# Sixteen output stores issued by ScalarE instead of SyncE in a four-layer graph network kernel

## The chip, the core and the metric

The kernel runs on one core of a Trainium2 chip. A core has TensorE (PE, matmuls; its weight loads are listed as PEld), VectorE (DVE), ScalarE (ACT), GpSimd (POOL) and SyncE (SP), which here only issues DMAs. Each engine works through its own instructions in the order of the program and waits on semaphores for the others. SP and ACT can both issue DMAs; their issuing sides are listed as SPq and ACTq. The metric is the device time of one execution in microseconds (us).

## What is computed

Sixteen graphs of 512 nodes with 128 features go through four attention layers with one shared adjacency matrix. Each layer's result is added to its input and normalised over the features:

```
x = _layernorm(x + _L0_gnn_ref(x, adj, ...))   # 4-head dot-product attention, masked
x = _layernorm(x + _L1_gnn_ref(x, W, a, adj))  # additive (GAT) attention
x = _layernorm(x + _L2_gnn_ref(x, adj, adj[None], ...))  # 8-head GAT with a prior
x = _layernorm(x + _L3_gnn_ref(x, adj, ...))   # MLP, GAT without mask, MLP, GAT with mask
return x                                        # (16, 512, 128) float32
```

The graphs do not depend on each other. Everything is float32 except the two masks.

## The kernel before

A graph's 512 nodes lie as 128 partitions x 4 blocks (C = 4). A layer is cut into stages, for instance `l0_exp` (one exponential of a 128x512 tile of scores) or `l3_norm` (the last normalisation of a graph, four ACTIVATEs of 128x128 at L811). The order of all stages on each engine is written out in the table ORDER: two characters a step, the stage's letter from STAGES and the graph's number in hexadecimal. So K5 in ACT's list is `l3_norm` of graph 5. Several graphs are under way at once, in different layers; PE's list is the densest. A stage waits for what it reads, and for buffers and PSUM banks that it overwrites.

SP's list has loads of a graph's input (`x_load`, L419, tile x_in), the write of a small row table to DRAM (`l2_rows`, L427), eight loads for each graph that spread one row of it over all partitions (`l2_spread`, L434, tile row, five buffers), which DVE reads in `l2_p` (L1230), and until now one `store` for each graph (L423, 256 KB from tile x4 to the output). The store waits for the semaphore l3_x, which the fourth ACTIVATE of `l3_norm` raises:

```
sp.wait_ge(*sig("l3_x", g, 1))
sp.dma_start(out_v[g.i], g.of(x4)[:, :, :]).then_inc(g.of(stored), 16)
```

Tile x4 has two buffers. ACT's `l3b_v` writes one for graph g once the store of graph g - 2 has landed. The program ends when SP has seen all stores land.

The PE stages named below, with what they wait for: `l0_pv` (L522) needs ACT's `l0_t` (L776); the stages at L572 need ACT's three small exponentials (L801 to L803); the projections at L554 need ACT's copy of the transposed input (L748); L616 needs ACT's copy at L834; the scores at L503 need banks that ACT or DVE has emptied. A stage named "warm" (L701) is two matmuls without use in front of a stage that would otherwise find PE idle.

Of the kernel before, what the change touches and what calls it, by code (L numbers as in the profile page):

```python
# [30 lines left out]


STAGES = {
# [55 lines left out]
        "l4i5l4v2a7D1w2w2E1E1b7x2m4x2x2d6x2d6n4d6e6o4d6o4j5e6e6d6e6y2d6c7d6p4F1e6d6r3e6e6K0e6f6f6d6d6d6d6A2H1"
        "H1I1J1t3A2A2A2B2C2d6u3d6l5r4v3e6l5e6d6e6d6e6e6D2w3e6w3f6e6m5x3x3x3x3n5E2E2o5o5K1e6y3d7r4d7d7p5d7f6e7"  # L90
        "A3e7d7e7d7e7d7e7g6A3e7d7h6A3i6A3e7B3e7C3i6t4d7f7d7f7d7F2d7e7e7e7a8e7j6b8f7u4d7c8d7e7d7H2e7H2e7I2d7J2"
        "r5v4e7l6f7l6D3w4w4x4x4m6x4E3x4E3n6o6g7o6K2d8r5d8y4d8h7e8d8e8i7e8i7d8e8d8e8d8a9F3A4p6d8t5e8j7A4d8d8d8"
        "A4d8A4e8b9e8f8u5e8B4e8C4e8v5e8l7l7H3H3f8I3f8J3c9d8d8d8d8r6e8m7e8e8e8D4w5w5f8x5x5x5x5n7E4E4o7o7y5g8K3"
        "r6h8d9aad9i8d9e9i8F4p7d9A5d9e9j8e9d9e9d9A5e9baA5d9e9t6A5B5C5d9H4d9e9u6H4e9d9e9l8e9l8e9I4cav6J4f9d9f9"
        "r7m8e9D5f9w6w6n8E5E5x6x6o8o8x6d9x6d9d9e9d9e9y6e9e9daF5dadar7dap8f9K4eaeaeaeadafadaabdaeadaeag9H5daA6"
        "H5h9daA6dai9I5daA6i9eaJ5eaeaA6B6C6dar8dabbeadaeafaeadaeaeafaeaeacbj9t7faD6E6E6u7v7dbdbw7l9w7dbgal9x7"
        "dbx7F6x7x7ebebebhaebK5dbm9r8y7dbn9dbiao9ebo9dbebiaebdbebdbfbdbdbA7dbp9A7dbjaA7dbA7dbebt8ebB7ebC7ebfb"
        "fbebebebebfbu8laH6lav8acH6I6J6r9bcmaD7w8gbw8E7naE7hbccoax8x8x8x8iboaibK6y8dcjbdcr9dcpadcececececaddc"
        "dcA8dcF7ecdcA8A8ect9ecA8ecB8C8dcdcdcdcH7u9H7lbbdeclbecI7ecdcecdcJ7v9rafcdcecmbecfcecD8fcw9dcw9E8nbE8"
        "ecx9x9fcobobx9x9K7y9cdgcrahcpbicicaeddA9ddedddjcddedF8ededA9ddA9ddedddddedbeededA9ddtaddedddfdddB9H8"  # L100
        "C9ualcH8lcedvaedI8edfdJ8ddddddrbfdddedmcededD9edwawafdncxaxaocK8ocxaxaE9E9cegdF9yarbpchdididafdeH9de"
        "dedeAaH9eeI9eeJ9eeeeAaAadeAadejddeeetbdeeebfeecffedeBadeCaeedeubrceeldeevbeedeeeldfefeDawbwbEadeEade"
        "mdeexbeexbnddexbdexbeeK9eeoddfoddfdfdfrcdffedfefdfefdfefefeftcefgeefybefdfdfpdhedfdfieFaieAbucdfjeAb"
        "dfvcdfdfAbffAbBbCbHaefefHaefIaefJaleleffffefefefrdefmeDbKaffnewcwcoeoexcxcxcxcEbEbycgfrdhfpeififFbjf"
        "ActdAcHbudHbAclfIblfAcvdJbBcCcremfnfofofDcwdwdEcEcxdxdxdxdFcreydpfKbteHcueAdAdveAdAdBdCdHcIcJcrfDdwe"
        "weEdEdxexexexeyeFdrfKctfAeAeAeAeBeCeHdHdufIdJdvfDewfwfEeEeKdxfxfxfxfFeyfHeAfAfAfAfBfHeCfIeJeDfEfEfKe"
        "FfHfHfIfJfKf",
    "dve":
        "00a0b0b0b0b0c000b020b030b040b050c0001000b060b0a1b0b0c0b0b0b0b0c0b1b1b1b1c1d0e0b1b1b1b1c1f0b1b1g0b1h0"
        "b1i0b1c1b1b1b1c1a2b2j0b2b2b2k0c2d1l0e1b2b2n0b2n0b2n0c2f1n0b2b2b2o0b2g1c2h1i1o0b2b2p0b2q0b2c2j1a3k1l1"  # L110
# [33 lines left out]
        "jfpeqeretdvcwcxcpfqfrfvdwdxdtevewexetfvfwfxf",  # L144
    "sp":
        "a0001000a1300000a2a3f0a4g0g0g0g0g0g0g0g0f1g1a5g1g1g1g1g1g1g1f2a6g2g2g2g2g2g2g2g2f3g3g3a7g3g3g3g3g3g3"
        "f4g4g4l0g4g4g4g4g4g4l1f5g5a8g5g5g5g5g5g5g5a9l2f6g6g6g6g6g6g6g6g6aal3f7g7g7g7g7g7g7g7g7f8g8l4abg8g8g8"
        "g8g8g8g8acl5f9g9g9g9g9g9g9adg9g9l6fagagagagagagagagaael7fbgbgbgbgbgbgbgbgbl8affcgcgcgcgcgcgcgcgcl9fd"
        "gdgdgdgdgdgdgdgdlafegegegegegegegegefflbgfgfgfgfgfgfgfgflcldlelf",
}  # L150
BANK_OF_USE = (
    "01234567012345670157021635635437504632017465312704635120743152047320641752306754172305647301526743021654723106"
# [55 lines left out]
def build_program(nc, x, adj, w, out):  # L208
    use = bank_uses()

    with ExitStack() as ctx:
        def sb(name, shape, dt=F32):
            return ctx.enter_context(nc.sbuf_tensor(name, shape, dt))

        def pair(name, shape, dt=F32, n=2):
            return [sb(f"{name}_{q}", shape, dt) for q in range(n)]
# [79 lines left out]
        x4 = pair("x4", [P, C, D])  # L296
        e4 = sb("e4", [P, C, D])
# [9 lines left out]
        stored = [sem(f"stored{q}") for q in range(2)]  # L307
# [44 lines left out]
        def emptied(stage, g, k=0):  # L352
            return bank_read[use[stage, k, g.i][0]]
# [17 lines left out]
        out_v = out.rearrange("b (p c) d -> b p c d", c=C)  # L371
# [13 lines left out]
        def _(sp):  # L385
# [32 lines left out]
                    sp.wait_ge(*took("l0_y", g, back=2))  # L418
                sp.dma_start(g.of(x_in)[:, :, :], x_v[g.i]).then_inc(g.of(x_loaded), 16)  # L419

            def store(g, k):
                sp.wait_ge(*sig("l3_x", g, 1))
                sp.dma_start(out_v[g.i], g.of(x4)[:, :, :]).then_inc(g.of(stored), 16)  # L423

            def l2_rows(g, k):
                sp.wait_ge(*sig("l2_turned", g, 1))
                sp.dma_start(g.of(line2).rearrange("r (q s) -> q r s", s=BLOCK), turned2[:, :]).then_inc(signal["l2_rows"], 16)  # L427
# [284 lines left out]
        def _(act):  # L712
# [175 lines left out]
            def elu_first(n, e, parts):  # L888

                def f(g, k):  # L890
                    for c in range(parts):
                        act.wait_ge(*took(n + "_o", g, c))
                    act.activation(e[:, :, :], e[:, :, :], ACT.Exp, scale=-1.0).then_inc(signal[n + "_ea"], 1)  # L893
                return f

            def elu_second(n, e):
                def f(g, k):
                    act.wait_ge(*sig(n + "_ea", g, 1))
                    act.activation(e[:, :, :], e[:, :, :], ACT.Exp, bias=neg_one[:, 0:1]).then_inc(signal[n + "_eb"], 1)  # L899
# [23 lines left out]
            def l2_old(g):  # L923
# [509 lines left out]
```

## Time and profile before

| | us |
|---|---|
| three runs, median (lowest to highest) | 1078.31 (1078.24 to 1078.61) |
| the profiled execution, its own time | 1080.22 |
| its span, first to last instruction | 1078.4 |
| PE busy | 1024.1 (95%) |
| PE weight loads busy | 760.1 (70%) |
| DVE busy | 914.3 (85%) |
| ACT busy | 771.2 (72%) |
| POOL busy | 272.7 (25%) |

The profile is of one execution. A busy engine may still be one that waits between pipelined instructions, and idle time of an engine that does not set the pace costs nothing. In a row of the timeline the first number is the start in us from the span's start, the second the time until the row's last instruction ends; "x4" means that four instructions are merged in it, and square brackets give the idle time before it and what ended that.

### The profile page before, as it was taken

The numbers are of one execution on the slowest core, as the hardware profiler recorded it, in microseconds if no ns is written. First come the engines' busy times: TensorE is split into PE (matmuls) and PEld (weight loads), VectorE is DVE, ScalarE is ACT, GpSimd is POOL, SyncE is SP. The second block draws the span as 40 slices with busy tenths as digits, with TensorE's granted clock in tenths as the row PEclk, the third lists the DMA queues.
The fourth block names the chain that finished last, engine by engine and source line by source line (L and its number), as shares of the span: only waits on it lengthen the run. The fifth ranks groups of instructions, "written<-read, shape, count | busy, mean of one in ns | idle before, by whom it ended". The sixth has DMA issues, their size and how long they took to land. (4 is left out here: it accounts for less than half of the span.)

```text
span 1078.4 us, 26660 instructions
## 1 busy us (share of the span) xinstructions
PE 1024.1 (95%) x9189; PEld 760.1 (70%) x9189; DVE 914.3 (85%) x2533; ACT 771.2 (72%) x2029; POOL 272.7 (25%) x606
## 2 busy tenths in 40 slices
PE   7989999999999999999999999999999999899985
PEld 5667767667677777868577776777676777666784
DVE  4656999998999988999899799989899798988543
ACT  3979858775777788768886977868867875544543
POOL 1012414131323224222212332223213232220101
PEclk9999999999999999999999999999999999999998
DMA  4000212202020200202030031112020021020000
GB/s 127 2 11 12 90 29 63 70 21 76 16 78 14 90 11 21 80 22 79 2 100 11 12 90 56 35 33 69 21 80 2 25 67 60 30 72 19 11 11 20
DMA packets 30468, 46.81 MB, mean 43 GB/s; under 512 B 6912, under 2 KB 9216, under 8 KB 30336
## 3 DMA queue, kind: packets, MB, share of 16 engines
q1 hardware_dynamic: 29472, 44.84, 13.4%
q8 instruction: 76, 1.25, 0.5%
q14 instruction: 56, 0.46, 0.1%
q10 hardware_dynamic: 864, 0.26, 0.1%
HBM read 40.64 MB, written 4.46 MB: 42 GB/s over the span
## 5 line engine op out<-in xcount | busy, mean ns | idle before, releaser
L1230 DVE SCALAR_TENSOR_TENSOR P<-row,t2e,mask_t 128x512 f32<-128x512 f32 x512 | 355.9, 755 | 11.2 <-PE bank L608 10.4
L766 ACT ACTIVATE probs<-probs,neg_max 128x512 f32<-128x512 f32 x256 | 186.7, 732 | 35.6 <-DVE neg_max L1046 35.6
L1038 DVE CUSTOM_DVE_ANT_0 probs<-bank,mask_add 128x512 f32<-128x512 f32 x256 | 169.5, 677 | 20.4 <-PE bank L503 19.8
L776 ACT ACTIVATE probs_t<-bank 128x512 f32<-128x512 f32 x256 | 151.0, 610 | 12.7 <-PE bank L511 12.2
L511 PE MATMUL bank<-ident,probs 128*128 128x128 f32 x1024 | 142.7, 277 | 5.1 <-ACT probs L766 3.1
L511 PEld LDWEIGHTS bank<-ident,probs 128*128 128x128 f32 x1024 | 114.0, 141 | 37.5 <-ACT probs L766 19.9
L811 ACT ACTIVATE x<-x,shift_l,rstd_l 128x128 f32<-128x128 f32 x256 | 105.3, 487 | 38.9 <-POOL shift_l L1368 38.9
L608 PE MATMUL bank<-P,GH 128*32 128x512 f32 x1024 | 116.4, 595 | 4.5 <-issue 3.2
L653 PE MATMUL bank<-t,l_P 128*128 128x258 f32 x512 | 119.8, 383 | 1.0 <-DVE l_P L1152 0.9
L1353 POOL TENSOR_TENSOR rstd_l<-mv_l,ln_eps 128x4 f32<-128x4 f32 x64 | 16.1, 252 | 384.0 <-DVE mv_l L1092 383.8
L653 PEld LDWEIGHTS bank<-t,l_P 128*128 128x128 f32 x512 | 93.8, 190 | 16.7 <-issue 2.5
L1386 POOL TENSOR_TENSOR t<-t 128x128 f32<-128x128 f32 x128 | 55.5, 465 | 169.1 <-ACT t L803 169.1
L608 PEld LDWEIGHTS bank<-P,GH 128*32 128x32 f32 x1024 | 31.7, 109 | 67.1 <-issue 64.7
L503 PE MATMUL bank<-head_k,head_q 32*128 32x512 f32 x512 | 72.7, 638 | 1.2 <-ACT probs_t L776 0.8
L1361 POOL TENSOR_TENSOR rstd_l<-rstd_l,neg_half 128x4 f32<-128x4 f32 x64 | 70.5, 1102 | 4.2
L522 PE MATMUL bank<-probs_t,v 128*32 128x128 f32 x2048 | 68.1, 275 | 0.4 <-DVE row_max L1038 0.4
L522 PEld LDWEIGHTS bank<-probs_t,v 128*32 128x32 f32 x2048 | 52.7, 109 | 21.7 <-issue 11.7
L584 PE MATMUL bank<-t,l_P 128*128 128x129 f32 x512 | 62.3, 276 | 0.0
L584 PE MATMUL bank<-t,l3b_P 128*128 128x130 f32 x512 | 61.5, 276 | 0.8 <-DVE l3b_P L1136 0.8
L584 PEld LDWEIGHTS bank<-t,l_P 128*128 128x128 f32 x512 | 59.4, 192 | 4.0 <-DVE l_P L1136 1.9
L584 PEld LDWEIGHTS bank<-t,l3b_P 128*128 128x128 f32 x512 | 59.2, 191 | 2.7 <-DVE l3b_P L1136 1.3
L644 PE MATMUL bank<-w_fc,h_t 128*128 128x258 f32 x256 | 60.2, 383 | 0.9 <-DVE row_max L1038 0.9
(168 smaller groups left out, 1922.5 us busy)
## 6 DMA issues: line engine op xcount, KB each, us to landing
row<-line SPq DMA_DIRECT2D x128, 256.0 KB, 3.7
x_in<-in_x SPq DMA_DIRECT2D x16, 256.0 KB, 2.8
out<-x SPq DMA_DIRECT2D x16, 256.0 KB, 2.0
l_P<-in_adj SPq DMA_DIRECT2D x4, 256.0 KB, 5.2
w_fc<-in_L_gnn_W_fc SPq DMA_DIRECT2D x1, 256.0 KB, 4.2
P<-in_L_gnn_a_fc SPq DMA_DIRECT2D x1, 256.0 KB, 3.5
line<-turned SPq DMA_DIRECT2D x16, 16.0 KB
w_cat<-in_L_gnn_W SPq DMA_DIRECT2D x2, 64.0 KB, 4.1
```

The costliest lines, as they stand in the source:

```text
L503: pe.matmul(ps("l0_s", g, HEADS0 * c + h)[:, :], g.of(head_q)[rows, c * P:(c + 1) * P], g.of(head_k)[rows, :], start=True, stop=True)\
L511: last = pe.transpose(ps[:, j * P:(j + 1) * P], probs[m // HEADS0 % 2][:, m % HEADS0, j * P:(j + 1) * P], ident[:, :])
L522: last = pe.matmul(ps[DH0 * h:DH0 * (h + 1), 0:P], g.of(v0)[:, j, DH0 * h:DH0 * (h + 1)], probs_t[c % 2][:, h, j, :], start=(j == 0), stop ...
L584: last = pe.matmul(ps[:, c * width:(c + 1) * width], gat[n]["P"][:, j, (2 * k + c) * P:(2 * k + c + 1) * P], g.of(t)[:, j, 2:2 + width], s ...
L608: last = pe.matmul(ps[DH0 * h:DH0 * (h + 1), :], g.of(GH)[:, j, (GROUP2 * q + h) * W2:(GROUP2 * q + h) * W2 + DH0], P2[:, h, j, :], start= ...
L653: last = pe.matmul(ps[:, 0:HID + 2], gat["l3"]["P"][:, j, c * P:(c + 1) * P], g.of(t3)[:, j, 2:4 + HID], start=(j == 0), stop=(j == C - 1))
L766: act.activation(e, e, ACT.Exp, bias=neg_max[:, m:m + 1], scale=SCALE0, accum_out=g.of(den0)[:, m:m + 1])\
L776: act.activation(probs_t[c % 2][:, h, :, :].rearrange("p j n -> p (j n)"), ps("l0_t", g, m)[:, :], ACT.Copy)\
L811: last = act.activation(y[:, c, :], y[:, c, :], ACT.Identity, bias=shift[n][:, c:c + 1], scale=rstd[n][:, c:c + 1])
L1038: dve.tensor_tensor_reduce(probs[c % 2][:, h, :], ps("l0_s", g, m)[:, :], mask_add[:, c, :], 1.0, -3.0e38, ALU.add, ALU.max, row_max[:, m: ...
L1230: last = dve.scalar_tensor_tensor(P2[:, h % GROUP2, j, :], row(g, h)[:, :], g.of(t2e)[:, j, h:h + 1], mask_t[:, j, :], ALU.max, ALU.mult)
L1361: pool.tensor_tensor(rstd[n][:, :], rstd[n][:, :], neg_half[:, :], ALU.pow)\
```

## The change

The stage `store` leaves SP's list and comes into ACT's as letter L, for each graph directly behind that graph's K (`l3_norm`). Its wait and its DMA are the same, but ACT now executes them. All other steps of all lists keep their order.

```diff
 STAGES = {
-    "sp": "0:adj_load 1:late_loads 3:out_load a:x_load f:l2_rows g:l2_spread l:store",
+    "sp": "0:adj_load 1:late_loads 3:out_load a:x_load f:l2_rows g:l2_spread",
...
-           "I:l3b_ea J:l3b_eb K:l3_norm",
+           "I:l3b_ea J:l3b_eb K:l3_norm L:store",
...
-            def store(g, k):
-                sp.wait_ge(*sig("l3_x", g, 1))
-                sp.dma_start(out_v[g.i], g.of(x4)[:, :, :]).then_inc(g.of(stored), 16)
...
+            def store(g, k):
+                act.wait_ge(*sig("l3_x", g, 1))
+                act.dma_start(out_v[g.i], g.of(x4)[:, :, :]).then_inc(g.of(stored), 16)
```

SP at the first two stores, graphs 0 and 1, before. The names in brackets are the semaphores that a step waits for; p2_made tells that DVE has used a row buffer:

```order
L427 DMA line_0<-turned 4x32x32 [waits l2_turned]
L434 DMA row<-line_0 128x512 [waits p2_made,l2_rows]
L434 DMA row<-line_0 128x512 [waits p2_made]
L423 DMA out<-x_0 128x512 [waits l3_x]
L434 DMA row<-line_0 128x512 [waits p2_made] x6
L423 DMA out<-x_1 128x512 [waits l3_x]
L427 DMA line_1<-turned 4x32x32 [waits l2_turned]
```

And now:

```order
L423 DMA line_0<-turned 4x32x32 [waits l2_turned]
L430 DMA row<-line_0 128x512 [waits p2_made,l2_rows]
L430 DMA row<-line_0 128x512 [waits p2_made] x7
L423 DMA line_1<-turned 4x32x32 [waits l2_turned]
L430 DMA row<-line_1 128x512 [waits p2_made,l2_rows]
```

Both waits for l3_x are gone from between the row loads (the function's removal also moves the line numbers by four).

ACT around `l3_norm` of graph 5 (near 603 us in the trace), before:

```order
L811 ACTIVATE x_1<-x_1,shift_l,rstd_l 128x128 [waits l3_shift]
L811 ACTIVATE x_1<-x_1,shift_l,rstd_l 128x128 x3
L766 ACTIVATE probs,den_1<-probs,neg_max 128x512 [waits neg_max0]
L811 ACTIVATE x_1<-x_1,shift_l,rstd_l 128x128 [waits l1_shift]
L811 ACTIVATE x_1<-x_1,shift_l,rstd_l 128x128 x3
L834 ACTIVATE o_raw<-bank 128x512 [waits bank_written0]
```

And now:

```order
L807 ACTIVATE x_1<-x_1,shift_l,rstd_l 128x128 [waits l3_shift]
L807 ACTIVATE x_1<-x_1,shift_l,rstd_l 128x128 x3
L900 DMA out<-x_1 128x512 [waits l3_x]
L762 ACTIVATE probs,den_1<-probs,neg_max 128x512 [waits neg_max0]
L807 ACTIVATE x_1<-x_1,shift_l,rstd_l 128x128 [waits l1_shift]
L807 ACTIVATE x_1<-x_1,shift_l,rstd_l 128x128 x3
```

One DMA stands between the normalisation and the exponential that followed it at once, and it waits for the normalisation in front of it.

ACT at `l3_norm` of graph 14 (near 1057 us), before:

```order
L790 ACTIVATE t_0<-bank 128x2x130 [waits bank_written2,bank_written1]
L811 ACTIVATE x_0<-x_0,shift_l,rstd_l 128x128 [waits l3_shift]
L811 ACTIVATE x_0<-x_0,shift_l,rstd_l 128x128 x3
L801 ACTIVATE l3b_R<-l3b_ss 128x4 [waits bank_read4,l3b_dd]
L802 ACTIVATE l3b_b<-l3b_dd 128x4
```

And now:

```order
L786 ACTIVATE t_0<-bank 128x2x130 [waits bank_written2,bank_written1]
L807 ACTIVATE x_0<-x_0,shift_l,rstd_l 128x128 [waits l3_shift]
L807 ACTIVATE x_0<-x_0,shift_l,rstd_l 128x128 x3
L900 DMA out<-x_0 128x512 [waits l3_x]
L797 ACTIVATE l3b_R<-l3b_ss 128x4 [waits bank_read4,l3b_dd]
L798 ACTIVATE l3b_b<-l3b_dd 128x4
```

Here graph 14's store has come in front of the three small exponentials of graph 15, the last graph.

## Rows read from the trace of the kernel before

**Rows 1.** The page's first part: busy us of each engine.

```profile
PE 1024.1 (95%) x9189; PEld 760.1 (70%) x9189; DVE 914.3 (85%) x2533; ACT 771.2 (72%) x2029; POOL 272.7 (25%) x606
```

**Rows 2.** Busy time by stretch: PE, PEld, DVE, ACT, POOL; granted clock.

```profile
600.00:660.00 60.00, 59.88 (x555) 44.49 (x557) 52.48 (x147) 47.88 (x125) 15.94 (x38) 1.00 0.16 46
...
940.00:950.00 10.00, 10.00 (x40) 6.82 (x38) 8.59 (x18) 4.64 (x10) 0.00 (x0) 0.86 0.01 2
...
1020.00:1078.00 58.00, 44.26 (x294) 37.34 (x291) 23.85 (x67) 23.88 (x63) 7.96 (x22) 0.95 0.04 15
```

**Rows 3.** Waits of SP's queue: total us, times, longest.

```profile
SPq L423 <- ACT x L811: 264.5, 16, 37.4
```

**Rows 4.** DVE's reads of tile row, 300 to 1000 us: what its idle before them ended on.

```profile
  PE bank L608: 6.3, 6
```

**Rows 5.** Timeline of DVE, its one wait for a row's DMA in the whole span.

```profile
268.07 2.08 DVE L1230 SCALAR_TENSOR_TENSOR P<-row,t2e,mask_t 128x512 f32<-128x512 f32 x3 [0.74 <-DMA row<-line]
```

**Rows 6.** Tile x_in: first and last start of its reads by PE.

```profile
L470 PEld LDWEIGHTS bank<-ident,x_in x64: 137/142/230, 4.5 to 788.7; 128*128 128x128 f32 x64
```

**Rows 7.** Timeline, ACT's DMA issues at the start.

```profile
0.73 0.41 ACTq L716 DMA_DIRECT2D l3b_P<-in_L_gnn_wq  x1
1.17 0.46 ACTq L716 DMA_DIRECT2D l3b_P<-in_L_gnn_wk  x1
```

**Rows 8.** SP's DMA issues: ns shortest, median, longest; first and last start.

```profile
L423 SPq DMA_DIRECT2D out<-x x16: 332/338/344, 311.6 to 1075.6; - x16
...
L434 SPq DMA_DIRECT2D row<-line x128: 319/430/1556, 114.5 to 973.5; - x128
```

**Rows 9.** Timeline at the store of graph 0, ACT and PE's weight loads.

```profile
309.94 1.64 ACT L811 ACTIVATE x<-x,shift_l,rstd_l 128x128 f32<-128x128 f32 x4
311.48 0.58 ACT L776 ACTIVATE probs_t<-bank 128x512 f32<-128x512 f32 x1
...
312.36 0.81 PEld L522 LDWEIGHTS bank<-probs_t,v 128*32 128x32 f32 x32
```

**Rows 10.** Timeline behind the store of graph 2 (419.3 us).

```profile
421.25 0.21 ACT L803 ACTIVATE l_g<-l_dd 128x4 f32<-128x4 f32 x1
...
421.50 0.41 PEld L572 LDWEIGHTS bank<-ident,l_R 128*128 128x128 f32 x4
```

**Rows 11.** Timeline behind the store of graph 3 (482.0 us).

```profile
482.39 0.58 ACT L748 ACTIVATE xTl<-bank 128x512 f32<-128x512 f32 x1
...
483.04 0.53 PEld L554 LDWEIGHTS bank<-w_cat,xTl 128*128 128x128 f32 x4
```

**Rows 12.** Timeline behind the store of graph 4 (542.9 us).

```profile
543.95 1.10 ACT L776 ACTIVATE probs_t<-bank 128x512 f32<-128x512 f32 x2
...
545.44 0.34 PEld L503 LDWEIGHTS bank<-head_k,head_q 32*128 32x128 f32 x8 [0.56 <-issue]
```

**Rows 13.** Timeline behind the store of graph 5 (603.0 us).

```profile
606.57 0.58 ACT L748 ACTIVATE xTl<-bank 128x512 f32<-128x512 f32 x1
...
607.20 0.42 PEld L554 LDWEIGHTS bank<-w_cat,xTl 128*128 128x128 f32 x3
```

**Rows 14.** Timeline behind the store of graph 8 (776.5 us).

```profile
776.42 0.39 ACT L790 ACTIVATE t<-bank 128x288 f32<-128x288 f32 x1
...
776.90 0.21 DVE L1174 TENSOR_REDUCE d8max<-t 128x8 f32<-128x32 f32 x1
```

**Rows 15.** Timeline behind the store of graph 9 (841.3 us).

```profile
845.04 0.62 ACT L834 ACTIVATE o_raw<-bank 128x512 f32<-128x512 f32 x1
...
846.03 0.42 PEld L616 LDWEIGHTS bank<-ident,o_raw 128*128 128x128 f32 x4 [0.20 <-issue]
```

**Rows 16.** Timeline behind the store of graph 12 (1000.8 us).

```profile
1002.78 0.60 ACT L840 ACTIVATE O_t<-bank 128x512 f32<-128x512 f32 x1 [2.01 <-PE bank L470]
```

**Rows 17.** Timeline behind the store of graph 14 (1057.3 us).

```profile
1057.34 0.19 ACT L803 ACTIVATE t<-l3b_dd 128x4 f32<-128x4 f32 x1
...
1057.58 0.41 PEld L572 LDWEIGHTS bank<-ident,l3b_R 128*128 128x128 f32 x4 [0.25 <-ACT t L803]
```

More of the change, by code:

```diff
@@ L88 @@
         "E0w1w1f5x1m3j4x1x1n3x1e5e5o3o3e5e5f5y1f5d5d5d5F0r2d5e5p3e5A1e5e5A1f5A1H0H0A1t2I0g5J0b6c6B1C1h5r3u2i5"
[L89 to L107, printed above, removed]
+        "l4i5l4v2a7D1w2w2E1E1b7x2m4x2x2d6x2d6n4d6e6o4d6o4j5e6e6d6e6y2d6c7d6p4F1e6d6r3e6e6K0L0e6f6f6d6d6d6d6A2"
@@ new lines @@
+        "H1H1I1J1t3A2A2A2B2C2d6u3d6l5r4v3e6l5e6d6e6d6e6e6D2w3e6w3f6e6m5x3x3x3x3n5E2E2o5o5K1L1e6y3d7r4d7d7p5d7"
+        "f6e7A3e7d7e7d7e7d7e7g6A3e7d7h6A3i6A3e7B3e7C3i6t4d7f7d7f7d7F2d7e7e7e7a8e7j6b8f7u4d7c8d7e7d7H2e7H2e7I2"
+        "d7J2r5v4e7l6f7l6D3w4w4x4x4m6x4E3x4E3n6o6g7o6K2L2d8r5d8y4d8h7e8d8e8i7e8i7d8e8d8e8d8a9F3A4p6d8t5e8j7A4"
+        "d8d8d8A4d8A4e8b9e8f8u5e8B4e8C4e8v5e8l7l7H3H3f8I3f8J3c9d8d8d8d8r6e8m7e8e8e8D4w5w5f8x5x5x5x5n7E4E4o7o7"
+        "y5g8K3L3r6h8d9aad9i8d9e9i8F4p7d9A5d9e9j8e9d9e9d9A5e9baA5d9e9t6A5B5C5d9H4d9e9u6H4e9d9e9l8e9l8e9I4cav6"
@@ new lines @@
+        "J4f9d9f9r7m8e9D5f9w6w6n8E5E5x6x6o8o8x6d9x6d9d9e9d9e9y6e9e9daF5dadar7dap8f9K4L4eaeaeaeadafadaabdaeada"
+        "eag9H5daA6H5h9daA6dai9I5daA6i9eaJ5eaeaA6B6C6dar8dabbeadaeafaeadaeaeafaeaeacbj9t7faD6E6E6u7v7dbdbw7l9"
+        "w7dbgal9x7dbx7F6x7x7ebebebhaebK5L5dbm9r8y7dbn9dbiao9ebo9dbebiaebdbebdbfbdbdbA7dbp9A7dbjaA7dbA7dbebt8"
+        "ebB7ebC7ebfbfbebebebebfbu8laH6lav8acH6I6J6r9bcmaD7w8gbw8E7naE7hbccoax8x8x8x8iboaibK6L6y8dcjbdcr9dcpa"
+        "dcececececaddcdcA8dcF7ecdcA8A8ect9ecA8ecB8C8dcdcdcdcH7u9H7lbbdeclbecI7ecdcecdcJ7v9rafcdcecmbecfcecD8"
@@ new lines @@
+        "fcw9dcw9E8nbE8ecx9x9fcobobx9x9K7L7y9cdgcrahcpbicicaeddA9ddedddjcddedF8ededA9ddA9ddedddddedbeededA9dd"
+        "taddedddfdddB9H8C9ualcH8lcedvaedI8edfdJ8ddddddrbfdddedmcededD9edwawafdncxaxaocK8L8ocxaxaE9E9cegdF9ya"
+        "rbpchdididafdeH9dededeAaH9eeI9eeJ9eeeeAaAadeAadejddeeetbdeeebfeecffedeBadeCaeedeubrceeldeevbeedeeeld"
+        "fefeDawbwbEadeEademdeexbeexbnddexbdexbeeK9L9eeoddfoddfdfdfrcdffedfefdfefdfefefeftcefgeefybefdfdfpdhe"
+        "dfdfieFaieAbucdfjeAbdfvcdfdfAbffAbBbCbHaefefHaefIaefJaleleffffefefefrdefmeDbKaLaffnewcwcoeoexcxcxcxc"
@@ L108 @@
+        "EbEbycgfrdhfpeififFbjfActdAcHbudHbAclfIblfAcvdJbBcCcremfnfofofDcwdwdEcEcxdxdxdxdFcreydpfKbLbteHcueAd"
+        "AdveAdAdBdCdHcIcJcrfDdweweEdEdxexexexeyeFdrfKcLctfAeAeAeAeBeCeHdHdufIdJdvfDewfwfEeEeKdLdxfxfxfxfFeyf"
+        "HeAfAfAfAfBfHeCfIeJeDfEfEfKeLeFfHfHfIfJfKfLf",
     "dve":
@@ L146 @@
         "a0001000a1300000a2a3f0a4g0g0g0g0g0g0g0g0f1g1a5g1g1g1g1g1g1g1f2a6g2g2g2g2g2g2g2g2f3g3g3a7g3g3g3g3g3g3"
-        "f4g4g4l0g4g4g4g4g4g4l1f5g5a8g5g5g5g5g5g5g5a9l2f6g6g6g6g6g6g6g6g6aal3f7g7g7g7g7g7g7g7g7f8g8l4abg8g8g8"
-        "g8g8g8g8acl5f9g9g9g9g9g9g9adg9g9l6fagagagagagagagagaael7fbgbgbgbgbgbgbgbgbl8affcgcgcgcgcgcgcgcgcl9fd"
-        "gdgdgdgdgdgdgdgdlafegegegegegegegegefflbgfgfgfgfgfgfgfgflcldlelf",
+        "f4g4g4g4g4g4g4g4g4f5g5a8g5g5g5g5g5g5g5a9f6g6g6g6g6g6g6g6g6aaf7g7g7g7g7g7g7g7g7f8g8abg8g8g8g8g8g8g8ac"
+        "f9g9g9g9g9g9g9adg9g9fagagagagagagagagaaefbgbgbgbgbgbgbgbgbaffcgcgcgcgcgcgcgcgcfdgdgdgdgdgdgdgdgdfege"
+        "gegegegegegegeffgfgfgfgfgfgfgfgf",
 }
@@ L435, in l2_spread @@
                              .rearrange("(o n) -> o n", o=1).broadcast_to([P, N_NODES])).then_inc(row_done(g, h)[0], 16)
-            stages = {"x_load": x_load, "l2_rows": l2_rows, "l2_spread": l2_spread, "adj_load": adj_load, "out_load": out_load, "late_loads": late_loads, "store": store}
+            stages = {"x_load": x_load, "l2_rows": l2_rows, "l2_spread": l2_spread, "adj_load": adj_load, "out_load": out_load, "late_loads": late_loads}
             for name, g, k in turns("sp"):
@@ L944, in _ @@
                 "l3b_e": exps("l3b", 0.8, lambda g: g.of(t4)[:, :, D + 2]), "l3b_v": l3b_v,
-                "l3b_ea": elu_first("l3b", e4, 2), "l3b_eb": elu_second("l3b", e4), "l3_norm": normalise("l3", x4),
+                "l3b_ea": elu_first("l3b", e4, 2), "l3b_eb": elu_second("l3b", e4), "l3_norm": normalise("l3", x4), "store": store,
             }
```

## The prediction

> **What bounds the kernel now.** I read the page's busy times first. PE is busy 1024.1 of 1078.4 us, DVE 914.3, ACT 771.2 [rows 1]: PE sets the pace, and ACT has 28% of its time free. Then the busy time by stretch: in the middle of the kernel PE leaves almost nothing free (59.88 of 60 us from 600 to 660), while in the last 58 us it works 44.26, because only the last graphs are left and each engine waits for the next [rows 2]. So a delay of another engine costs time only if it makes PE late, and one that does in the middle finds nearly no idle time of PE to hide in. At the end every delay on the chain counts.
>
> Then SP's waits: 264.5 us in 16 waits for the stores' semaphore, the longest 37.4 us [rows 3]. This looks large, but SP does nothing else meanwhile. Whether it matters is seen at the readers of what SP loads behind a store. DVE, which reads the rows, sat idle for a row's DMA once, for 0.74 us at 268 us [rows 5], ahead of the first store (311.6 us [rows 8]). From 300 us on it only waited for PE at L608, six times, 6.3 us [rows 4]: that is for the buffer of P, not for a row. The last input load starts behind a store near 777 us and PE reads that tile at 788.7 at the latest [rows 6].
>
> **What is removed.** Sixteen waits and sixteen issues of 0.34 us [rows 8] on SP. Every one is hidden today, by the lead that the rows and inputs have over their readers. I take 0 us for it; the bound on the other side is the 0.74 us of row wait [rows 5], if I had placed it wrongly.
>
> **What is added, for one store on ACT.** Four parts. ACT overlaps its instructions: behind the store of graph 0 the next ACTIVATE starts at 311.48, while the normalisation ends at 309.94 + 1.64 = 311.58 [rows 9]. A DMA that waits for the end of the normalisation loses this overlap, 0.10 us. The semaphore takes some 0.02 us (SP's first issue starts at 311.6). The issue itself is not in the trace for ACT at this place. From below I take SP's issue of the same DMA, 0.34 us [rows 8]; from above ACT's own issues at the start, 0.41 and 0.46 us [rows 7]. Then 0.03 us until the next instruction (0.73 + 0.41 = 1.14 to 1.17 [rows 7]). This makes 0.49 to 0.61 us; I take 0.55, the middle, since ACT's own rows stand nearer to the case but were taken among other issues. It is 16 x 0.55 = 8.8 us of ACT time, 0.8% of the span, out of an engine with 28% free.
>
> The Trainium skill (DMA: Bandwidth & Descriptors, Issuing engines are not separate DMA queues) says that all issuing engines' DMAs run on the same 16 DMA engines and that the choice of issuer only moves the sequencer's issue time. By that page alone the price would be the issue, 0.34 us, without the drained pipeline, and the time near 1079.5; the first two rows of group 9 show the overlap that is lost as well.
>
> **What of it reaches PE.** ACT is late by 0.55 us until it next finds that much idle time. Meanwhile I look for the instruction of ACT that somebody waits for most closely. The gap between the end of ACT's instruction and the start of PE's weight load cannot fall below some 0.05 us (1057.34 + 0.19 = 1057.53 to 1057.58, where PE did wait [rows 17]). What is above this is slack.
> - Graph 0: 311.48 + 0.58 = 312.06 to 312.36 is 0.30, slack 0.25: PE late by 0.30 [rows 9].
> - Graph 2: 421.46 to 421.50, no slack: 0.55 [rows 10].
> - Graph 3: 482.97 to 483.04, slack 0.02: 0.53 [rows 11].
> - Graph 4: 545.05 to 545.44, slack 0.34; ACT had 0.07 us idle ahead: 0.14 [rows 12].
> - Graph 5: 607.15 to 607.20, none: 0.55 [rows 13].
> - Graph 9: 845.66 to 846.03, slack 0.32: 0.23 [rows 15].
> - Graph 14: no slack, and PE was waiting: 0.55, on the last graph's own chain [rows 17].
> - Graph 8 makes DVE late, not PE: 776.42 + 0.39 = 776.81 to 776.90, a gap of 0.09 us, nearly as close as the least for PE [rows 14]. It is worth 0 to 0.55 on PE; I take 0.2.
> - Graphs 1, 6, 7, 10, 11, 12, 13: ACT finds idle time before a close reader comes. Graph 12 is the clearest: 2.01 us idle directly behind the store [rows 16]. 0 us.
> - Graph 15: the last store is issued when its normalisation ends, as before; ACT's issue is up to 0.12 us longer than SP's. I take 0.05.
>
> **The sum.** Ahead of the end PE is late by 0.30 + 0.55 + 0.53 + 0.14 + 0.55 + 0.23 + 0.2 = 2.5 us. PE has idle moments in which part of this is lost again, where the thing waited for was not itself delayed: 0.12 us in 60 in the stretch from 600 to 660 [rows 2], more before 360 and after 900. Bounds: none absorbed, or all. I take a quarter absorbed, since three of the largest terms fall in the middle, where PE is nearly never idle: 1.9 us. With 0.55 + 0.05 at the end this is 2.5 us. The profiled span of 1078.4 becomes 1080.9, the profiled execution's own 1080.22 becomes 1082.7, and the median of 1078.31, which is what counts, becomes 1080.8. A measurement of this kernel can tell about 0.2%, 2.2 us, from no change, so the forecast is only just on the slower side.
>
> **The rivals.**
> - Nearly all is absorbed: the engines wait for each other so often that only the terms of the last graph stay, 0.55 + 0.05. Time 1078.9. For it: the small losses of 0.14 to 0.55 us are of the size of single idle moments. Against: 0.12 us of idle time in a whole 60 us stretch [rows 2].
> - ACT's issue is dearer than its rows at the start, because SP is spreading rows at the same moment: SP's own row issues go from 0.32 to 1.56 us [rows 8]. At 1.1 us for each store, 0.55 more at the seven places with PE late, 3.9 us more, and places with slack between 0.5 and 1.0 us join. Time about 1085.
> - The clock: from 940 to 950 us the granted clock is 0.86 in the mean, which is a piece at 1.2 instead of 2.4 GHz; PE was busy all that time [rows 2]. 14% of 10 us, 1.4 us, could be given back if work behind shifts such that this piece does not occur, or come a second time. Time 1079.4 or 1082.2. Nothing in the trace says which.
> - Faster: SP, freed from holding its queue, fetches rows sooner, and DVE and with it PE go ahead. It decides only if more than 2.5 + 2.2 = 4.7 us of the 6.3 us that DVE waited before row reads [rows 4] were in truth waits for rows held behind a store. If all were, 6.3 less 2.5 us are won: 1074.5. Against it: the profile names PE for all six, and the only wait that it names a row for has no store in front [rows 5].
>
> The Trainium skill (Perfetto Trace Analysis, DMA Optimizations) advises one issuing engine for inputs and another for outputs. What it would do here is the last rival, and the most that it could give is that rival's time; no row shows a reader that waits behind a store.
>
> **How the numbers follow.** Chances: the forecast, delays that mostly stay, 0.5, from 1079.8 to 1082.3; nearly all absorbed 0.25; dearer issue 0.12; the clock piece, mixed with either, 0.08; faster 0.05. The predicted time is 1080.8. The range goes down to all absorbed and some of the clock piece given back, 1078.2, and up to nothing absorbed at 0.61 us for each with graph 8 whole, near 1082.2, and a part of the dearer issue, 1083.6. Slower by over 0.2% (above 1080.5): a bit over half of the forecast's share, the dearer issue and part of the clock's, 0.48. Within 0.2%: 0.45. Faster: 0.07.
>
> **What would show it.** ACTq should have 16 issues of 0.34 to 0.46 us, each starting 0.02 to 0.03 us behind the last normalisation, and the next ACTIVATE some 0.5 us later than now. PE's idle time for ACT should grow at L572, L554 and L522 by about half a microsecond at the places named, and the start of the same stage should drift late by steps: 0.3 at 312 us, about 0.8 at 425, 1.3 at 484, near 1.9 at 608. DVE's wait for rows should stay below 1 us. The prediction is wrong if the drift closes again between the places (absorbed), if ACTq's issues are long where SP is issuing rows, or if the drift goes negative behind a place where SP used to be held.

## The result, and the profile after

| | before | now |
|---|---|---|
| median of six runs each, us (lowest to highest) | 1078.46 (1077.74 to 1079.78) | 1083.71 (1081.99 to 1084.36) |
| ratio now to before, 95% interval | | 1.0043 (1.0030 to 1.0056) |
| profiled execution, its own time | 1080.22 | 1082.4 |
| its span | 1078.4 | 1080.2 |

The changed kernel is slower by 0.43%. On the 1078.31 us that the prediction started from this is 4.6 us (3.2 to 6.0), so some 1082.9 us, inside the predicted range of 1078.2 to 1083.6 and 2.1 us above the predicted 1080.8. The two medians themselves lie 5.25 us apart, and 1083.71 as it stands is 0.1 us above the upper end of the range. The predicted change was 2.5 us.

The profile of the changed kernel, first the busy times of the page; they hardly moved against [rows 1], since a DMA issue and a wait are not counted as busy:

```profile
PE 1023.3 (95%) x9189; PEld 758.6 (70%) x9189; DVE 915.1 (85%) x2533; ACT 771.6 (71%) x2029; POOL 273.5 (25%) x606
```

The busy time by stretch, in the columns of [rows 2]:

```profile
600.00:660.00 60.00, 59.60 (x551) 44.91 (x549) 52.25 (x149) 48.32 (x125) 16.26 (x39) 1.00 0.13 46
940.00:950.00 10.00, 8.63 (x40) 6.09 (x41) 10.00 (x20) 5.48 (x12) 0.00 (x0) 1.00 0.01 2
1020.00:1078.00 58.00, 45.04 (x299) 37.93 (x297) 24.55 (x68) 24.51 (x65) 7.98 (x22) 0.96 0.03 10
```

From 600 to 660 us PE now leaves 0.40 us free instead of 0.12. From 940 to 950 us the granted clock is 1.00 where it was 0.86, a difference that does not follow the stores, as the next section shows.

The DMA issues by line, in the columns of [rows 8]. L900 is the store, now on ACT's queue, L430 the spreading of rows that stayed on SP:

```profile
L900 ACTq DMA_DIRECT2D out<-x x16: 338/338/353, 311.1 to 1077.4; - x16
...
L430 SPq DMA_DIRECT2D row<-line x128: 315/430/1534, 113.4 to 974.8; - x128
```

ACT's issue is as short as SP's was. None of the sixteen ran while SP was issuing a row, though; one, graph 4's, met the start of an input load's issue for 0.01 us. SP's waits, in the columns of [rows 3]:

```profile
SPq L423 <- DVE turned L1217: 429.0, 16, 54.9
...
SPq L437 <- DMA out<-x: 104.4, 1, 104.4
```

The wait for the stores' semaphore is gone, and SP waits for the next thing instead, DVE's `turned`. What DVE's reads of the rows waited for from 300 to 1000 us, as in [rows 4]:

```profile
  PE bank L604: 6.3, 6
```

Not a hundredth less than before. Ahead of 300 us, and so ahead of every store, DVE waited for a row's DMA twice: for 0.73 us near 268 us, as before in [rows 5], and for 0.66 us at 118 us, 1.4 us together where the prediction expected less than 1. The next section comes back to the one at 118 us. Now ACT at the store of graph 0, a timeline, which answers to [rows 9]:

```profile
311.14 0.35 ACTq L900 DMA_DIRECT2D out<-x  x1
311.54 0.60 ACT L772 ACTIVATE probs_t<-bank 128x512 f32<-128x512 f32 x1 [0.43 <-ACT x L807]
...
312.19 0.48 PEld L518 LDWEIGHTS bank<-probs_t,v 128*32 128x32 f32 x20 [0.42 <-ACT probs_t L772]
```

The normalisation ended at 311.12 us. The issue starts 0.02 us later, and the next ACTIVATE starts 0.42 us behind the end of the normalisation, where in [rows 9] it started 0.10 us before that end. PE then waits 0.42 us for `probs_t`, which it did not wait for in [rows 9]. At the end of the program, graph 14's store in front of the exponentials of the last graph, which answers to [rows 17]:

```profile
1058.52 0.34 ACTq L900 DMA_DIRECT2D out<-x  x1
1058.95 0.20 ACT L797 ACTIVATE l3b_R<-l3b_ss 128x4 f32<-128x4 f32 x1 [0.47 <-ACT x L807]
1059.16 0.19 ACT L799 ACTIVATE t<-l3b_dd 128x4 f32<-128x4 f32 x1
...
1059.40 0.30 PEld L568 LDWEIGHTS bank<-ident,l3b_R 128*128 128x128 f32 x3 [0.84 <-ACT t L799]
```

PE waited 0.25 us there before and 0.84 us now, 0.59 more.

### The profile page after: what moved, and what is told of

Read it like the earlier page. It is cut to its first block and busy times, and to the rows that moved or that the text cites. A ratio compares the mean times of both kernels' runs of the same rounds, so it can differ in the third digit from the quotient of the medians.

```text
span 1080.2 us, 26660 instructions
## 1 busy us (share of the span) xinstructions
PE 1023.3 (95%) x9189; PEld 758.6 (70%) x9189; DVE 915.1 (85%) x2533; ACT 771.6 (71%) x2029; POOL 273.5 (25%) x606
## 5 line engine op out<-in xcount | busy, mean ns | idle before, releaser
L499 PE MATMUL bank<-head_k,head_q 32*128 32x512 f32 x512 | 72.7, 638 | 1.3 <-ACT probs_t L772 1.2
```

The lines of the kernel that those rows point to most:

```text
L499: pe.matmul(ps("l0_s", g, HEADS0 * c + h)[:, :], g.of(head_q)[rows, c * P:(c + 1) * P], g.of(head_k)[rows, :], start=True, stop=True)\
```

## Where the time went: the drift between two traces

The most telling reading here is a subtraction of starts. The orders of PE's instructions are the same in both kernels, so each one's start in one trace can be set against its start in the trace of before. The difference, the drift, stays level where nothing happens and makes a step where a delay reaches PE. The steps at each graph's store, in us, with PE's lines numbered as in the kernel before:

| store of graph | predicted | now | now, a second trace | where PE was held |
|---|---|---|---|---|
| 0 | 0.30 | 0.30 | 0.29 | L522, by ACT |
| 2 | 0.55 | 0.57 | 0.59 | L572, by ACT |
| 3 | 0.53 | 0.57 | 0.59 | L616, then L554, by ACT |
| 4 | 0.14 | 0 | 0 | L503, by ACT, but made up at once |
| 5 | 0.55 | 0.52 | 0.54 | L470, then L554, by ACT |
| 7 | 0 | 0.01 | 0.01 | |
| 8 | 0.2 | 0.41 | 0.41 | L563, by DVE |
| 9 | 0.23 | 0.54 | 0.54 | L616 by ACT, L542 by DVE |
| 10 | 0 | 0.35 | 0.38 | L563, by DVE |
| 14 | 0.55 | 0.59 | 0.60 | L572, by ACT |
| 1, 6, 11, 12, 13, 15 | 0.05 | 0 | 0 | |
| absorbed again | -0.6 | 0 | 0 | |
| sum | 2.5 | 3.86 | 3.95 | |

The larger part of the step came at an earlier reader than the one predicted at graph 3 (0.47 of 0.57 us at L616) and at graph 5 (0.35 of 0.52 us at L470, which reads the next normalisation's result).

The spans differ by less, 1080.2 - 1078.4 = 1.8 us. Two other differences account for it. The execution profiled for the new kernel reached 300 us, before any store, 0.47 us ahead of the one before. And between 937 and 945 us the drift falls by 1.67 us. The stretch around that, in the trace of before and then in that of the changed kernel (columns as in [rows 2]):

```profile
935.00:950.00 15.00, 12.78 (x58) 9.12 (x56) 13.59 (x26) 6.88 (x15) 0.97 (x2) 0.89 0.00 1
```

```profile
935.00:950.00 15.00, 11.53 (x64) 7.81 (x57) 14.73 (x32) 8.21 (x17) 2.65 (x4) 1.00 0.01 2
```

A mean of 0.89 over 15 us is a piece of 3.3 us at 1.2 GHz, which costs half of that, 1.65 us; PE is busy 12.78 us for 58 matmul instructions there, against 11.53 us for 64. The profile of before had this piece and that of the changed kernel did not. So 3.86 - 0.47 - 1.67 = 1.7, and 1.8 is what the spans show. The piece does not follow the stores: of the nine traces below, whatever their stores did, eight are without it at that place and one (e5) has it. The two profiled spans alone would have given 1.8 us for a change that costs 4 to 5.

The 0.47 us ahead of 300 us is itself a sum. At 65 us the drift falls by 1.2 us: the trace of before has a piece at the lower clock there too (granted clock 0.83 from 60 to 70 us, against 1.00 now). At 118 to 126 us it rises by 0.6 us, behind a wait for a row that before does not have:

```profile
118.14 2.74 DVE L1230 SCALAR_TENSOR_TENSOR P<-row,t2e,mask_t 128x512 f32<-128x512 f32 x4 [0.66 <-DMA row<-line]
```

Such a wait of 0.23 to 0.90 us, with a step of 0.15 to 0.8 us on PE, stands at that place in the trace of the changed kernel and in those of e2, e4, e5, e7, e8 and e9, and not in those of before, e1, e3 and e6. Up to there the engines' orders are the same in all kernels. No experiment was made on it, and the step is not in the table.

## The experiments

The theory after the result: the price is made at nine places, each with about half a microsecond of lateness of ACT (wait for its own last instruction, issue, restart), next to none of it absorbed, and some of it carried to PE by DVE. The rivals: the stores of the other graphs or the queue of SP have a part in it; the issue itself is the price, wherever it stands; the wait alone is the price; the engines' small idle moments absorb most and something else makes up the sum. All kernels compute the whole function. "Timed" ratios are to the kernel before on the same chip, with 95% intervals.

**e1_free7: ACT stores only the graphs where no PE delay was seen.** Graphs 1, 6, 7, 11, 12, 13 and 15 are stored by ACT as in the change, the other nine by SP at their old places.

```diff
# SP's list
-f4g4g4g4g4g4g4g4g4f5g5a8...a9f6...aaf7...
+f4g4g4l0g4g4g4g4g4g4f5g5a8...a9l2f6...aal3f7...
# ACT's list
-K0L0e6f6 ... K1L1e6y3 ... K2L2d8r5
+K0e6f6   ... K1L1e6y3 ... K2d8r5
```

> ScalarE issues the stores of graphs 1, 6, 7, 11, 12, 13 and 15 directly behind their normalisation, SyncE the other nine as before. Theory A (a store costs what its place lets through to PE): nothing, within 0.5 us of before, since ACT finds idle time behind each of the seven. Theory B (every store on ACT costs the same share of the loss of some 4.6 us, 0.29 us each): 2.0 us slower. Theory C (the loss comes from using a second DMA queue at all, wherever): most of the 4.6 us.

Timed: 1077.54 against 1076.96 us, ratio 1.0004 (0.9995 to 1.0014). The drift has no step above 0.05 us at a store between 300 and 937 us. ACT is late by 0.46 to 0.58 us behind the stores of graphs 1, 6, 7 and 13 and not at all behind those of 11 and 12, where it sat idle anyway; none of it reaches PE.

**e2_close9: ACT stores only the other nine** (0, 2, 3, 4, 5, 8, 9, 10, 14), the complement in both lists:

```diff
# ACT's list
-K1L1e6y3 ... K6L6y8dc ... K7L7y9cd
+K1e6y3   ... K6y8dc   ... K7y9cd
```

> The complement: ScalarE issues the stores of graphs 0, 2, 3, 4, 5, 8, 9, 10 and 14, SyncE the other seven. Theory A: the whole loss of the changed kernel, 4 to 5 us over before, in steps of 0.3 to 0.6 us at these graphs. Theory B: 9 x 0.29 = 2.6 us.

Timed: 1081.68 against 1076.96 us, ratio 1.0046 (1.0032 to 1.0060), the same as the whole change. The steps are 0.30, 0.59, 0.57, 0, 0.53, 0.41, 0.54, 0.35, 0.59: sum 3.88. So the nine are the whole price, and with e1 the two parts add up: 1.0004 and 1.0046 against 1.0043.

**e3_idle: all sixteen on ACT, each moved away from its normalisation**, to the first later stage with over 0.65 us of idle time in front of it in the trace of before (graph 15 at the end as now).

```diff
-K0L0e6f6f6 ... K1L1e6y3d7 ... K9L9eeod...ieFaieAb
+K0e6f6L0f6 ... K1e6y3L1d7 ... K9eeod...ieFaieL9Ab
```

> All sixteen stores on ScalarE, but each one put in front of the first later stage for which ACT sat idle for more than 0.65 us in the trace of before (graph 15's stays at the end). Theory A: as before, within 0.7 us; it is also the test of the rival that SyncE, freed of its waits, makes the rows earlier: if that is worth something, this kernel is faster than before. Theory B and C: as slow as the changed kernel, 4.6 us over before.

Timed: 1077.52 against 1076.96 us, ratio 1.0007 (0.9997 to 1.0018), and no step in the drift. This settles two rivals. The issues on ACT as such cost nothing that can be measured in 16 places, so it is the place. And SP's queue is as free of stores here as in the change, with no cost on the other side to hide a gain: none appears (by the interval, at most 0.3 us). DVE's reads of rows still waited the same 6.3 us in six times for PE. The idle time itself was hardly used: of the fifteen stores ahead of the last, thirteen were issued under a running ACTIVATE, as graph 0's:

```profile
310.69 0.58 ACT L772 ACTIVATE probs_t<-bank 128x512 f32<-128x512 f32 x1
310.82 0.35 ACTq L900 DMA_DIRECT2D out<-x  x1
311.17 0.27 ACT L779 ACTIVATE o_raw<-bank 128x128 f32<-128x128 f32 x1
```

So it is the distance from the normalisation that counts here, as e6 shows.

**e4_drain: the wait without the DMA.** SP stores as before; ACT has only the wait for l3_x at the sixteen places.

```diff
 def store(g, k):
     act.wait_ge(*sig("l3_x", g, 1))
-    act.dma_start(out_v[g.i], g.of(x4)[:, :, :]).then_inc(g.of(stored), 16)
```

> SyncE issues all stores as before, but ScalarE waits at the same sixteen places for its own normalisation to end, without issuing anything. The issue is left out of ACT's work, so ACT is late only by the lost overlap of 0.10 us, the semaphore's 0.03 and what a wait in front of the next instruction costs, 0.15 to 0.2 us in all. By slack at the places: graphs 2, 3, 5, 8, 9 and 14 pass on 0.1 to 0.2 us each, some 0.8 us over before. If the drain rather than the issue is the cost, the loss is most of the 4.6 us.

ACT's timeline at graph 2 in this kernel:

```profile
415.33 1.64 ACT L811 ACTIVATE x<-x,shift_l,rstd_l 128x128 f32<-128x128 f32 x4
417.00 0.72 ACT L766 ACTIVATE probs<-probs,neg_max 128x512 f32<-128x512 f32 x1
```

and the same place in the kernel before:

```profile
417.63 1.65 ACT L811 ACTIVATE x<-x,shift_l,rstd_l 128x128 f32<-128x128 f32 x4
419.17 0.72 ACT L766 ACTIVATE probs<-probs,neg_max 128x512 f32<-128x512 f32 x1
```

The exponential started 0.11 us before the end of the normalisation and now starts 0.03 us behind it: the wait alone costs 0.14 us. PE's steps are 0.14, 0.13, 0.13, 0.15 and 0.14 at graphs 2, 3, 5, 9 and 14, sum 0.7. Timed: 1079.16 against 1076.96 us, ratio 1.0016 (1.0007 to 1.0026), which is 1.7 us (0.8 to 2.8), more than the steps explain. The direction is clear, the size of the rest is not (this trace also has the step near 118 us, 0.6 us).

**e5_twice: the cost doubled.** Each store is two DMAs of 128 KB.

```diff
-act.dma_start(out_v[g.i], g.of(x4)[:, :, :]).then_inc(g.of(stored), 16)
+for q in range(2):
+    act.dma_start(out_v[g.i][:, 2*q:2*q+2, :], g.of(x4)[:, 2*q:2*q+2, :]).then_inc(g.of(stored), 16)
```

> As the changed kernel, but each store in two DMAs of 128 KB, so two issues on ScalarE at each place. The second issue adds some 0.34 + 0.04 us. Theory A: the eight places that passed on 0.30 to 0.59 us in the changed kernel's trace pass on about 0.38 us more each, 3.0 us, and places whose slack was between 0.6 and 1.0 us join (graphs 1, 4, 6 by their idle gaps of 0.66 to 0.7): 7 to 8 us over before. If the cost were a fixed one of each place (the wait or the drain), it stays at 3.8 to 5 us.

The page's issue line and graph 0 in the timeline of this kernel:

```profile
L901 ACTq DMA_DIRECT2D out<-x x32: 338/346/1115, 310.5 to 1083.4; - x32
```

```profile
310.50 0.84 ACTq L901 DMA_DIRECT2D out<-x  x2
311.38 0.60 ACT L772 ACTIVATE probs_t<-bank 128x512 f32<-128x512 f32 x1 [0.91 <-ACT x L807]
```

The ACTIVATE waits 0.91 us where it waited 0.43. The second issue took 0.45 us, not 0.34, here and at thirteen other stores; it took 1.115 us at graph 7 and 0.34 us at graph 14, where it started 0.32 us behind the end of the first. The steps became 0.78, 1.05, 1.05, 0.16, 1.01, 0.89, 1.01, 0.85 and 1.24 at graphs 0, 2, 3, 4, 5, 8, 9, 10 and 14, 0.47 to 0.65 more than with one DMA at each of them but graph 4. There PE was late by 0.58 us and made up 0.41 of it within 5 us, which leaves 0.16. Graph 7, with the long issue, joined with 0.78, of which 0.18 was made up later, and 0.13 more was made up at 668 us. Graphs 1 and 6, expected to join, did not. Sum about 8.5, where 7 to 8 had been expected. Timed: 1087.57 against 1077.76 us, ratio 1.0092 (1.0073 to 1.0110). With e8 beside it on the same chip, the second DMA costs 0.0044 x 1078 = 4.7 us, as in the traces (8.5 - 3.95 = 4.6). So an added lateness of ACT reaches PE at full size at eight of the nine places, which speaks against much absorption there; some 0.7 us were made up elsewhere.

**e6_issue_late: the DMA without the wait.** ACT issues the store of graph g - 1 behind the normalisation of graph g, so that l3_x has long been raised (graph 14's, which has to come sooner, stands in front of `l3b_v` of graph 15).

```diff
-K0L0e6f6 ... K1L1e6y3 ... K2L2d8r5
+K0e6f6   ... K1L0e6y3 ... K2L1d8r5
```

> Behind the normalisation of graph g ScalarE issues the store of graph g - 1, whose data have long been ready (graph 14's goes in front of graph 15's attention copy, graph 15's to the end). The sixteen issues stay, the wait for the own pipeline goes. If ScalarE's issuing side can work on the DMA while the last ACTIVATE still runs, the next one is late by 0.1 us or less instead of 0.58, and the kernel is within 0.8 us of before. If a DMA issue is only begun when ScalarE is empty, the loss stays at 3 us or more.

Timed: 1078.17 against 1077.76 us, ratio 1.0003 (0.9993 to 1.0012), no step in the drift. The timeline of ACT at the store of graph 0, which is now behind the normalisation of graph 1:

```profile
350.34 0.49 ACT L807 ACTIVATE x<-x,shift_l,rstd_l 128x128 f32<-128x128 f32 x1 [1.22 <-POOL shift_l L1368]
350.35 0.35 ACTq L900 DMA_DIRECT2D out<-x  x1
350.74 1.25 ACT L807 ACTIVATE x<-x,shift_l,rstd_l 128x128 f32<-128x128 f32 x3
351.90 0.57 ACT L772 ACTIVATE probs_t<-bank 128x512 f32<-128x512 f32 x1
```

In the program the DMA stands behind four ACTIVATEs, but it is issued while the first of them has only begun, 1.64 us before the last one ends, and the next ACTIVATE overlaps that end by 0.09 us as it did in the kernel before. At all of the fifteen stores ahead of the last the next ACTIVATE starts as it did before, to 0.02 us. ACT's issuing side is ahead of its arithmetic, and the 0.35 us lie under it. So neither the issue alone (0) nor the wait alone (0.7) makes the 3.9 us of steps: the wait holds the issuing side until the arithmetic is done, and only then does the issue lie bare.

**e7_only14: graph 14 alone on ACT**, one run.

```diff
-...K0L0... (16 stores in ACT's list)
+...KeLeFf... (one store in ACT's list, fifteen in SP's)
```

> Only the store of graph 14 is on ScalarE. In the trace the same stage of TensorE should be as in before's up to 1057 us, apart from the start-up, and 0.55 to 0.6 us late from then to the end; nowhere else a step.

One run, 1079.01 us beside a median of 1077.76; a single run says nothing at this size. The trace does. ACT at the store:

```profile
1055.38 0.35 ACTq L904 DMA_DIRECT2D out<-x  x1
1055.84 0.21 ACT L801 ACTIVATE l3b_R<-l3b_ss 128x4 f32<-128x4 f32 x1 [0.48 <-ACT x L811]
```

The drift goes from -1.91 to -1.29 us, a step of 0.62, whatever the fifteen others do. A slow creep of 0.3 us between 300 and 937 us without a step at a store is not explained; it is about the accuracy of the method.

**e8_after_again: the changed kernel once more**, unchanged, beside e5 and e6.

> The changed kernel once more, to see how often the pieces at half clock fall: its steps by graph should repeat to within 0.05 us (sum 3.8 us), and the time be 4 to 5 us over before. If the steps differ from run to run, the theory of fixed places is wrong.

Timed: 1083.46 against 1077.76 us, ratio 1.0048 (1.0031 to 1.0065). Steps in the table above, each within 0.03 us of the first trace.

**e9_two_later: the two places carried by DVE.** Graph 9's store moves behind both `l2_h` of graph 13, graph 10's one step down, behind `l0_ov`; one run.

```diff
-K9L9eeoddfod ... KaLaff
+K9eeoddfodL9 ... KaffLa
```

> The changed kernel, with only two stores moved by a few steps: graph 9's behind both copies of the layer 2 projection of graph 13 (four steps later), graph 10's behind the last copy of graph 15's attention output (one step later), so that VectorE's L1174 and L1066 are served before ScalarE issues. If these two steps of the drift (0.54 and 0.38 us) come by VectorE being late, graph 9's falls to 0.2 us or less (the part that TensorE's L616 waits for ScalarE's own copy) and graph 10's to about 0, with all other steps as before. If ScalarE's own lateness passes to TensorE directly, both stay.

One run, 1081.83 beside 1077.58 us. In the trace the step at graph 9 goes from 0.54 to 0.01, that at graph 10 from 0.38 to 0, and the others stay; the sum is 2.98 instead of 3.9. ACT in this kernel around the store of graph 9:

```profile
843.66 0.61 ACT L772 ACTIVATE probs_t<-bank 128x512 f32<-128x512 f32 x1
843.82 0.34 ACTq L900 DMA_DIRECT2D out<-x  x1
844.14 0.44 ACT L786 ACTIVATE t<-bank 128x288 f32<-128x288 f32 x1
```

Again the issue lies under running ACTIVATEs, because what it waited for had ended at 843.79 us, while other work stood between. A few stages of distance, not the whole way of e3, were enough, and more of graph 9's step went than I had expected. Graph 10 is the cleaner test of the way over DVE:

```profile
895.40 0.34 ACTq L900 DMA_DIRECT2D out<-x  x1
895.84 0.60 ACT L744 ACTIVATE xTl<-bank 128x512 f32<-128x512 f32 x1 [0.31 <-issue]
```

ACT is still 0.42 us late behind this store, but the copy that DVE reads now stands ahead of it, and PE's step is gone.

## Why the prediction was right, and where its sum was short

**The bound, and SP.** Right. DVE waited the same 6.3 us before its rows with a free SP queue, and e3 and e6, which have that queue without the cost on ACT, are at 1.0007 and 1.0003: nothing was to be gained, by the intervals at most 0.3 and 0.8 us. The rival "faster" falls. The Trainium skill (Perfetto Trace Analysis, DMA Optimizations) says that it may make sense to give inputs to one issuing engine and outputs to another; this case's runs show no gain from it where the stores stand well (e3, e6) and a loss where they don't.

**One store's price on ACT.** Right. 0.02 us of semaphore, 0.338 us of issue, 0.05 to 0.10 us to the next ACTIVATE and some 0.10 us of lost overlap (the wait alone, overlap and restart, was 0.14 in e4). ACT was late by 0.52 to 0.58 us behind eleven stores, against the predicted 0.55, by 0.40 and 0.45 at graphs 4 and 7, where it had no overlap to lose, and by 0 at graphs 11 and 12. The upper end, from ACT's own issues at the start [rows 7], was not reached; SP's row was the better guide.

**Dearer issues beside SP's rows.** Not seen: 338 to 353 ns in all 16. But in the changed kernel none of them ran while SP was issuing a row, so it does not test the rival. In e3, e5 and e6 four did; they took 361, 338, 363 and, as a second DMA, 450 ns, at most 25 ns more than others of their kind. The 1.115 us issue of e5 had no issue of SP beside it.

**The places where ACT releases PE.** Right, and to hundredths: 0.30, 0.57, 0.57, 0.52 and 0.59 against 0.30, 0.55, 0.53, 0.55 and 0.55, though at graphs 3 and 5 most of it fell at an earlier reader. At graph 4 PE's L503 (now L499) was released by DVE before and is released by ACT now:

```profile
545.47 1.14 PE L503 MATMUL bank<-head_k,head_q 32*128 32x512 f32 x8 [0.35 <-DVE row_max L1038]
...
546.63 1.14 PE L499 MATMUL bank<-head_k,head_q 32*128 32x512 f32 x8 [0.41 <-ACT probs_t L772]
```

The drift was 1.06 us ahead of it and is 1.16 here, so 0.1 us late where 0.14 was predicted. PE's next stage waits for DVE, which was not late, and the 0.1 us was gone 1.1 us later.

**The step that failed: "I take a quarter absorbed".** Of the predicted terms only graph 4's was, 0.1 us, and nothing of the steps in the table. Beside them PE was late once by 0.25 us, at L554 behind graph 10's store, and made it up within 0.5 us; in e5 some 0.7 of over 9 us were made up. Why the idle moments that I counted as room for it gave none, no experiment shows; the likely reason is that they ended on work of ACT or of DVE that was itself late, and so moved along. That is 0.6 us of the 3.86 - 2.5 = 1.36 that were missing in the sum.

**The term that was mis-sized: what DVE carries.** I looked for the instruction of ACT that PE waits for most closely and, but for graph 8, not for the chain from ACT over DVE to PE. Graph 9 in the trace of before:

```profile
843.16 0.21 DVE L1174 TENSOR_REDUCE d8max<-t 128x8 f32<-128x32 f32 x1 [0.44 <-issue]
...
847.50 1.16 PE L542 MATMUL bank<-woT,o_t 128*128 128x128 f32 x8
```

and in that of the changed kernel:

```profile
843.32 0.34 ACTq L900 DMA_DIRECT2D out<-x  x1
...
845.69 0.21 DVE L1174 TENSOR_REDUCE d8max<-t 128x8 f32<-128x32 f32 x1 [0.96 <-issue]
...
848.24 0.66 PE L612 MATMUL bank<-ident,o_raw 128*128 128x128 f32 x4
...
850.03 1.16 PE L538 MATMUL bank<-woT,o_t 128*128 128x128 f32 x8 [0.26 <-DVE o_t L1066]
```

The drift is 2.00 us ahead of the store. At L616 (now L612) it is 848.24 - 846.03 [rows 15] = 2.21, the 0.2 that I had predicted from ACT. But DVE's L1174 is at 2.53, and 0.33 us more reach PE that way at L538. Graph 10 is the same, from 893.45 and 901.11 us before:

```profile
893.45 0.68 DVE L1066 TENSOR_TENSOR o_t<-bank,o_raw 128x512 f32<-128x512 f32 x1
...
901.11 0.27 PE L563 MATMUL bank<-ident,l_dmax 128*128 128x128 f32 x1
```

```profile
895.41 0.34 ACTq L900 DMA_DIRECT2D out<-x  x1
896.36 0.69 DVE L1066 TENSOR_TENSOR o_t<-bank,o_raw 128x512 f32<-128x512 f32 x1 [0.28 <-ACT o_raw L779]
...
903.95 0.32 PE L559 MATMUL bank<-ident,l_dmax 128*128 128x128 f32 x1
```

DVE waits 0.28 us for ACT, which it did not before, and PE is late by 0.30 us here and by 0.35 from its next instruction on. Graphs 8, 9 and 10 are 0.41 + 0.54 + 0.35 = 1.30 us against the 0.43 predicted, 0.87 of the missing 1.36. (The 0.6 and the 0.87 together are 0.11 too much: graph 4 gave 0.14 less than predicted, the rest is hundredths.) I had set graph 10 to nothing because ACT finds idle time before a close reader on PE comes; DVE was closer.

**The range.** That the measurement lies inside it is in part luck. The upper end of 1083.6 us held a part of the dearer issue, which did not come. Without it, with nothing absorbed and graph 8 whole, I had 1082.2, below the 1082.9 measured, since what DVE carries at graphs 9 and 10 was in no term.

**The clock.** Such pieces are real, and they do not follow the change: one worth 1.7 us stood in the profiled execution of before at 939 us and near the same place in that of e5, and in none of the others there. It took 1.7 us from the difference of the profiled spans.

**The issue time as the whole price.** Behind a wait for ACT's own last result a store makes ACT 0.52 to 0.58 us late, and with that wait already satisfied it costs 0. The Trainium skill (DMA: Bandwidth & Descriptors, Issuing engines are not separate DMA queues) says that starting DMAs on several engines only saves the issue time on the sequencer. Read as a price, that would be the measured 0.34 us in both cases, an estimate; the runs differ from it on both sides.

**What stays open.** Timed, the change costs 4.6 and 5.2 us in two comparisons, in the steps 3.9; the lower ends of the intervals (3.2 and 3.3 us) hold that, and e4 and e5 too were 1 us or more over their steps when timed. Two things on record could fill the gap. With the step near 118 us the traces come to 4.5 and 4.8 us for the changed kernel and 1.3 for e4; but whether the timed executions have it, and whether it belongs to these kernels or to chance, no run tells. And the mean granted clock of the timed executions was 0.9946 in e8 against 0.9955 in the kernel before beside it, a difference of 0.001 or 1 us. The start of the program up to 300 us moved by +0.01 (e9) to -3.14 us (e1) between executions, and no experiment was made to hold it still. No version beat the kernel before; e1, e3 and e6 equal it.

## What to carry to other kernels

When an instruction is put behind a wait for the same engine's last result, price three things: the drained overlap and the restart (0.14 us together in e4) and the issue (0.34 us), and look at who waits for that engine within the next few microseconds, over a third engine too. A DMA issue whose wait was already satisfied cost nothing here, so a store can stand on a busy compute engine if enough other work stands between it and the instruction that makes its data. Three small ACTIVATEs were enough at graph 6 in e3; one short copy, at graph 10 in e9, left ACT 0.42 us late. And when a change of a few microseconds is to be read from two profiles, subtract the starts of the same instructions and look for steps; the spans alone also carry the chance of clock and start-up.

## What the runs showed of the hardware that was not expected

- ACT's issuing side runs ahead of its arithmetic: a DMA behind four ACTIVATEs in the program was issued 1.64 us before the last of them ended, at no cost (e6).
- A second DMA straight behind the first on ACT took 0.45 us to issue at fourteen of sixteen stores, the first 0.338 to 0.353 (e5). One took 1.115 us, and one that started 0.32 us behind the end of the first took 0.338.
- ACT's issue of a 256 KB store took 338 to 353 ns, while single row issues of SP went up to 1534 ns in the same program; SP's median stayed at 430 ns, as in [rows 8]. The four store issues that ran beside a row issue of SP (e3, e5, e6) took at most 25 ns more than others.
- Single pieces of some 3.3 us at 1.2 GHz appear in one execution and not in the next of nearly the same program, each worth 1.7 us.
